# Attention in the middle of a fused macaron block: tokens normalised one batch ahead, products kept in their own batch, routing operands in PSUM, a third home for the probabilities

## The reference

```python
x = x + 0.5 * ffn(layernorm(x))
x = x + attention(layernorm(x))
x = x + 0.5 * ffn(layernorm(x))

# attention, for each batch b of 1024 tokens, width 128, causal
Q, K, V = x @ Qw, x @ Kw, x @ Vw
attn = softmax(Q @ K.T / sqrt(128) + causal_mask)
out = attn @ V

# ffn: 16 experts of 64, a router that takes 4 of 16 (from 2 of 4 groups), one shared expert of 128
scores = sigmoid(x @ Wg.T); cw = topk weights, scaled by 2.5
y = sum_e cw[:, e] * relu(x @ W1[e].T)**2 @ W2[e].T + relu(x @ Ws1.T)**2 @ Ws2.T
```

## Time and profile before

| | us |
|---|---|
| median of 3 runs (708.24 to 709.76) | 709.67 |
| the profiled execution's own time | 709.15 |
| its span, first to last instruction | 707.2 |
| PE busy in the span | 644.9 (91%) |
| DVE busy | 577.7 (82%) |
| ACT busy | 569.7 (81%) |
| POOL busy | 537.6 (76%) |

### The profile page before, as it was taken

One profiled execution on the slowest core, in us unless ns is written; L12 is line 12 of the kernel. 1 busy time (PEld: TensorE's weight loads), 2 busy tenths in 40 slices (PEclk: granted clock), 3 DMA queues, 4 the chain that ended last, 5 costly groups with the idle time before them and its releaser, 6 DMA issues.

```text
span 707.2 us, 15309 instructions
## 1 busy us (share of the span) xinstructions
PE 644.9 (91%) x3395; PEld 500.1 (71%) x3395; DVE 577.7 (82%) x2597; ACT 569.7 (81%) x1198; POOL 537.6 (76%) x427
## 2 busy tenths in 40 slices
PE   4789999999999997888888778689999999999997
PEld 4567777777777766676766666567777777777775
DVE  5998989898889895677687768988989898898863
ACT  3588889889888878888798767548898888888885
POOL 3389889989899876676556645547888998898885
PEclk9999999999999998899999999999999999999999
DMA  9857676677757712664555446953887778867783
GB/s 246 192 124 158 150 161 138 138 155 157 149 122 158 164 38 47 111 105 92 89 110 107 94 80 121 200 124 65 174 166 168 156 171 177 172 137 163 160 184 77
DMA packets 129305, 97.30 MB, mean 138 GB/s; under 512 B 80992, under 2 KB 94960, under 8 KB 129264
## 3 DMA queue, kind: packets, MB, share of 16 engines
q1 hardware_dynamic: 127056, 96.24, 66.6%
q10 hardware_dynamic: 2208, 0.59, 0.4%
HBM read 72.70 MB, written 5.24 MB: 110 GB/s over the span
## 4 chain that ended last, share of the span: by engine, by line
PE 38%; DVE 13%; ACT 5%; issue 4%; POOL 3%; DMA 1%; POOLq 0%; DVEq 0%; ACTq 0%; SPq 0%
PE psum L1319 10%; PE psum L1320 9%; PE psum L1321 9%; DVE raw_max L1190 4%; ACT zn L738 2%; PE psum L1392 2%; DVE x_sb L1223 1%; DMA wb<-scratch 1%; PE psum L1350 1%; POOL shared L518 1%; PE psum L1404 1%; PE psum L1543 1%; PE psum L1544 1%; PE psum L1545 1%; DVE s_sb L1059 1%
## 5 line engine op out<-in xcount | busy, mean ns | idle before, releaser
L430 POOL TENSOR_TENSOR shared_r<-shared,shared_r 128x512 fp32r<-128x512 f32 x256 | 326.7, 1299 | 54.2 <-ACT shared L614 51.9
L1059 DVE SCALAR_TENSOR_TENSOR s_sb<-psum,wb 128x512 f32<-128x512 f32 x256 | 175.6, 688 | 48.0 <-PE psum L1321 23.8
L614 ACT ACTIVATE shared<-s_sb 128x512 f32<-128x512 f32 x288 | 178.0, 620 | 23.1 <-DVE s_sb L1059 23.0
L613 ACT ACTIVATE shared_r<-s_sb 128x512 fp32r<-128x512 f32 x256 | 159.9, 624 | 42.0 <-DVE s_sb L1059 40.8
L518 POOL TENSOR_TENSOR shared<-s_sb,shared 128x128 f16<-128x128 f32 (+3 forms) x64 | 81.9, 1281 | 73.1 <-ACT shared L544 72.6
L1319 PE MATMUL psum<-x_hi,w_hi 128*128 128x512 f32 x288 | 127.9, 444 | 6.9 <-ACT s_sb L725 4.1
L1319 PE MATMUL psum<-shared_r,w_hi 128*128 128x512 f32 x256 | 115.1, 450 | 0.7 <-POOL shared_r L430 0.5
L1320 PE MATMUL psum<-x_lo,w_hi 128*128 128x512 f32 x288 | 115.4, 401 | 0.0
L1321 PE MATMUL psum<-x_hi,w_lo 128*128 128x512 f32 x288 | 114.3, 397 | 0.0
L1321 PE MATMUL psum<-shared_r,w_lo 128*128 128x512 f32 x256 | 101.4, 396 | 0.0
L1320 PE MATMUL psum<-shared_r,w_hi 128*128 128x512 f32 x256 | 101.1, 395 | 0.0
(11 more groups left out here) (198 smaller groups left out, 1387.7 us busy)
## 6 DMA issues: line engine op xcount, KB each, us to landing
wb<-scratch SPq DMA_DIRECT2D x128, 512.0 KB, 8.1
out<-x_sb SPq DMA_DIRECT2D x16, 256.0 KB, 9.9
x_sb<-in_L_attn_x SPq DMA_DIRECT2D x4, 256.0 KB, 6.1
scratch<-wT SPq DMA_DIRECT2D x32, 32.0 KB, 1.9
w_raw<-in_L_ffn_W ACTq DMA_DIRECT2D x1, 512.0 KB, 5.8
w_raw<-in_L_ffn_W SPq DMA_DIRECT2D x1, 512.0 KB, 6.8
w_raw<-shared SPq DMA_TRANSPOSE x32, 2.9
wb<-shared SPq DMA_TRANSPOSE x32, 3.9
```

Source lines behind the costliest of these rows:

```text
L430: nc.gpsimd.tensor_tensor(g_lo[:, j % RING, :], g_f[:, j % RING, :], g_hi[:, j % RING, :].bitcast(F32), ALU.subtract).then_inc(F.glo_done, 1)
L613: nc.scalar.activation(g_hi[:, j % RING, :], s_sb[:, j % RING, :], ACT.Square)
L614: nc.scalar.activation(g_f[:, j % RING, :], s_sb[:, j % RING, :], ACT.Square).then_inc(F.sq_done, 1)
L1059: ins = nc.vector.scalar_tensor_tensor(s_, h_, 0.0, wb[:, u, c, :], ALU.max, ALU.mult)
```

## The change

It touches attention, the groups of the second FFN that are started inside it, and where their operands lie.

- `zn` has two homes (the second in a part of `wb` that attention leaves free). ACT normalises all 8 tiles of batch b+2 at t = 0 of batch b, in one piece, for b = 1 to 5, and batches 1 and 2 inside batch 0. The statistics on DVE (t = 5 to 7) and the inverse root on POOL (t = 7) stand at the end of the batch before.
- The 16-bit high half of the tokens moves from ACT to POOL (`z16_halves`, a copy and a subtraction for each half batch), at t = 0 and 1.
- `mix(b, 0)` and `mix(b, 1)` run at t = 6 and 7 of their own batch (only batch 0's stay in batch 1). `values(b-2, 1)` moves from t = 7 to t = 0 of the next batch.
- `prob` has three homes instead of two, so `exp(m)` waits for `prob_lo(m-3)` instead of `prob_lo(m-2)`. `rsum` has three too.
- Batch b+1's q uses the same bank as its z (the spare bank 5 goes to the router), so `score(4)` waits for `q_lo_part` of half 0.
- The router's operands of groups 0 and 1 lie in PSUM bank 5, those of group 2 on in `v_ps`. The tables of k move, and groups 0 and 1 are transposed 2 and 9 tiles after they were normalised, in place of one. Their transposes and products go to `misc_ps`, and PE waits at t = 0 of batches 3 to 8 until that bank is read (`foreign`).

The diff, cut to its core:

```diff
+        prob_own = sb("prob", [P, S])
...
-        zn = sb("zn", [P, QT, D])
+        zn_own = sb("zn", [P, QT, D])
+        zn = [zn_own, wb[:, 0].rearrange("p c n -> p (c n)")[:, QT * D:2 * QT * D].rearrange("p (t d) -> p t d", t=QT)]
...
-        PF = 2
+        PF = 3
+        prob = [prob_s[:, 0:S], prob_s[:, S:2 * S], prob_own]
...
-        on_sb, on_ps = RouteTiles(rt_sb[:]), RouteTiles(v_ps)
+        on_ps, on_spare = RouteTiles(v_ps), RouteTiles(tr_ps)
...
-            z_home = psum[:, 1 + 2 * half, :]
-            return z_home, spare_ps if half == 0 and b < B - 1 else z_home
+            return psum[:, 1 + 2 * half, :]
...
+                def z16_halves(b, half):
+                    pool.wait_ge(A.zn_done, 2 * b + half + 1)
+                    wait(pool, A.mix_done, 4 * (b - 2))
+                    ts = slice(half * HQ, (half + 1) * HQ)
+                    z, z16 = zn[b % 2][:, ts, :], zn16[b % 3]
+                    nc.gpsimd.tensor_copy(z16[:, 0, ts, :], z).then_inc(A.z16hi_done, 1)
                     pool.wait_ge(A.z16hi_done, 2 * b + half + 1)
+                    nc.gpsimd.tensor_tensor(z16[:, 1, ts, :], z, z16[:, 0, ts, :], ALU.subtract).then_inc(A.z16lo_done, 1)
...
-                        if t == 5 and b + 2 < B:
-                            attention_inv(b + 2)
+                        if t == QT - 1 and b + 3 < B:
+                            attention_inv(b + 3)
                         prob_lo(b, t)
-                        if t in ((2, 3) if b > 0 else (3, 4)) and b + 1 < B:
-                            z16_lo(b + 1, t - (2 if b > 0 else 3))
+                        if b == 0 and t in (1, 2):
+                            z16_halves(0, t - 1)
+                        if b == 0 and t == 2:
+                            attention_inv(2)
+                        if b == 0 and t in (4, 5):
+                            z16_halves(1, t - 4)
+                        if 0 < b < B - 1 and t < 2:
+                            z16_halves(b + 1, t)
...
-                            if b == 0 and t < 2:
-                                normalise_tokens(1, t)
-                            if b + 1 < B and t in z16_at:
-                                z16_hi(b + 1, z16_at.index(t))
-                            if b + 2 < B and t >= 6:
-                                normalise_tokens(b + 2, t - 6)
+                                normalise_tokens(1)
+                            if t == 4 and b == 0:
+                                normalise_tokens(2)
+                            if t == 0 and 0 < b < B - 2:
+                                normalise_tokens(b + 2)
...
-                    for n, slots in ((0, {-23: (0,), -18: (1,), -17: (2,), -15: (3,), -10: (4,), -9: (5,), -7: (6,), -2: (7,), -1: (8,), 1: (9,)}),
+                    for n, slots in ((0, {-16: (0,), -14: (1,), -13: (2,), -8: (3,), -6: (4,), -5: (5,), -3: (6, 7), -2: (8,), 0: (9,)}),
...
-                                     (2, {14: (0, 1), 15: (2, 3), 16: (4, 5), 17: (6,)})) if phase == 1 else (
+                                     (2, {16: (0, 1), 17: (2, 3), 18: (4, 5), 19: (6,)})) if phase == 1 else (
...
+                            if t == 4 and 0 < b < B - 1:
+                                q_lo_part(b + 1, 1 - u, 1, prep_ps(b + 1, 1))
                             row_max(b, t, u)
...
+                            if t == 0 and 0 < b < B - 2:
+                                shift_by(b + 2)
+                            if t == 1 and b > 1:
+                                finish(b - 2, 1)
...
-                    if t == HQ + 1 and 0 < b < B - 1:
-                        pe.wait_ge(A.qlo_done, 2 * b + 4)
+                    if t in (HQ, HQ + 1) and 0 < b < B - 1:
+                        pe.wait_ge(A.qlo_done, 2 * b + t - 1)
+                    if t == HQ and b == B - 1:
+                        pe.wait_ge(N1.xf_done, 3)
...
+                            if 0 < b < B - 1 and t < 2:
+                                pe.wait_ge(A.exp_done, QT * b + t - 1)
+                                z_transpose(b + 1, 1 - u, t, prep_ps(b + 1, t))
+                            if b == 1 and t == 0:
+                                mix(0, 0)
+                                mix(0, 1)
+                            if t == 0 and b > 1:
+                                foreign(b)
+                                values(b - 2, 1)
+                            if t == 2 and b > 0:
+                                mix(b - 1, 2)
+                            if t in (2, 3) and 0 < b < B - 1:
+                                q_product(b + 1, 1 - u, t - 2, prep_ps(b + 1, t - 2))
+                            if t == 3 and b > 0:
+                                values(b - 1, 0)
+                            if t in (4, 5) and b > 0:
+                                mix(b - 1, 3, t - 4)
+                            if t in (6, 7) and b > 0:
+                                mix(b, t - 6)
```

More of the change, by code:

```diff
@@ L790, in run @@
                         sc.wait_ge(A.pT_in[r], 16 * 2 * B)
-                    for c in range(AHEAD - 1):
+                    lead_ffn(0)
+                    start_ffn(17)
+                    for c in range(1, AHEAD):
                         lead_ffn(c)
                     uT_copy(B - 1, 1)
-                    lead_ffn(AHEAD - 1)
                 return begin, run
@@ L884, in ffn, with mv_home @@
                 N_ROUTE = sum(STEPS)
-                def home(g, beyond):
-                    return on_sb if phase == 1 and isinstance(g, int) and g <= beyond else on_ps
+                def mv_home(g):
+                    return rt_mv[:] if phase == 1 and isinstance(g, int) and g <= PREP else on_ps.mv
                 def bias_copy(tiles):
@@ L921, in route @@
                     score = scores[:, u]
-                    T = home(g, PREP - 2)
-                    first_on_ps = PREP - 1 if phase == 1 else 0
+                    T = on_spare if phase == 1 and isinstance(g, int) and g < UN else on_ps
+                    first_on_ps = UN if phase == 1 else 0
                     def do(ins):
@@ L1276, in run @@
[L1276 to L1283 removed]
+                            if t in (1, 2) and b == 0:
+                                stats(2, t - 1)
@@ L1607, in run @@
                             if b > 0:
                                 start_ffn((b - (B - 2)) * QT + t)
-                    b, u = B - 1, (B - 1) % UN
-                    mix(b, 0)
-                    mix(b, 1)
+                    b = B - 1
+                    foreign(B)
+                    values(b - 1, 1)
+                    pe.wait_ge(A.exp_done, QT * B - 1)
+                    lead_ffn(0)
+                    lead_ffn(1)
+                    start_ffn(16)
                     pe.wait_ge(A.exp_done, QT * B)
-                    lead_ffn(0)
+                    lead_ffn(2)
```

247 lines of the change are left out of this document (111 added, 136 removed).

## The result

The changed kernel is slower: 724.6 us (median of 4 runs, 723.1 to 725.1) against 709.2 for the kernel before (4 runs beside them on the same chip, 708.2 to 709.8). The ratio is 1.0215, interval 1.0194 to 1.0235. The forecast was 701.7, range 690 to 710. The profiled execution took 723.09 us, its span 721.3; before it was 709.15 and 707.2.

The account below looks back on a forecast made before the run. No engine fills a batch: waits in the loop score, maximum, exponential and a slower PE clock bound it. From 709.15 us, +3.0, -2.8, -4.4, -4.6 and +1.0 make -7.8: 701.4, with 0.5 about 701.7; range 690 to 710.

Parts of the forecast that it names:

- The shift: DVE's shift ahead of ACT's normalisation: behind `prob_lo(7)` in half of the batches, 1.5 us longer each, 0.75 on average.
- The end of the root, E + 2.4: POOL's inverse root, estimated from DVE's last maximum, 0.8 us of statistics and 1.64 us for the root.
- E: The start of a middle batch's last exponential, from which the prediction laid out the batch.
- The stop at q, 2.5 us: PE, through at E + 5.2, waits for z until E + 7.7, replacing the 1.93 us stop at the transpose.
- From q to the end of the batch, 15.1: PE's remaining work from E + 7.7: batch ends at E + 21.0, 22.5 with the slow stretch, plus 0.3 router work.
- Batches 2 to 5, 94.2 us: Four middle batches of attention, 97.0 us before, at 22.5 + 0.75 + 0.3 each: -2.8 us, bounds -12 to +2.
- The slow rival: Normalising eight tiles behind the late shift stops PE 4 us each batch; batches 2 to 5 at 24.6, about 716; chance 0.12.
- The router's groups: In batches starting a router group, PE's 2.26 us stop for tokens goes; 0.3 us of ACT's normalisation counted.
- Batches 0 and 1, +3: POOL's 16-bit halves, copies taken at 1.0 us, delay the roots in batch 0: +3 us, bounds 0 to +6.
- Batch 6, -4.4: No normalisation piece, so no stop at q: 21.5 us for 25.9, bounds -6 to -1.
- Batch 7, -4.6: Window loses about 4 us of DVE work, so PE bounds it: 20.0 us for 24.6, bounds -6 to -1.
- The tail, +1.0: After the last exponential, router group 2's parts stand before the second and third gate: +1.0 us, bounds 0 to +3.

Follow-up runs that it names:

- the moments in PSUM: The changed kernel with the means and variances of batches 2 to 7 in PSUM and no instruction moved: 714.4 us, ratio 1.0067.
- late pairs: The changed kernel with batches 1 to 5's shift at t = 2 and normalisation two tiles each at t = 3 to 6: 707.5 us, ratio 0.9976.
- the best version: Changed kernel with moments in PSUM, late pairs, router shifts two tiles later, mix pairs 0 and 1 back, router group 0's last part later: 694.4 us, ratio 0.9789.
- a version without the stops: Changed kernel with moments in PSUM, late pairs and router shifts two tiles later (698.4 us); two homes for the probabilities instead of three gave 700.6 us.

## Why the prediction was wrong, step by step

The step that failed is "The shift", and through it the layout of a middle batch. The wait for the shift was to be 1.5 us in half of the batches, 0.75 on average. It was 2.3 to 2.65 in every one.

- **The end of the root, E + 2.4.** It was E + 3.8 (E = 372.37). I timed the root by its input on DVE and left out what stands ahead of it in POOL's own queue: `prob_lo(6)`, 1.90 us, which can start only when ACT's copy of tile 6 is done, 0.1 us behind E. 0.1 + 1.9 + 1.64 was to be had before the run, from the order of the queues and the durations of the profile.
- **The shift late in half of the batches, 1.5 each.** With the root at E + 3.8 it was behind `prob_lo(7)` in every batch that has a root: ACT waited 2.65, 2.27, 2.65 and 2.50 us for it in batches 2 to 5. `prob_lo(7)` is ready at E + 2.3, as forecast, so the order of the two was no matter of chance. I had made it an even one.
- **The stop at q, 2.5 us.** It was 5.2, 3.4, 5.2 and 5.0 in batches 2 to 5. ACT's piece began at E + 5.97 for the E + 2.9 of the forecast. PE was through at E + 5.7 (forecast 5.2). Less ACT's wait for the shift, the stop is 2.5 in batches 2, 4 and 5. So up to the product q everything but the shift was right within 0.5.
- **From q to the end of the batch, 15.1 (13.3 at full clock, 1.5 for the slow stretch, 0.3 for the router's work).** It took 15.7 and 16.3 us in batches 4 and 5, and 16.6 and 17.3 in 2 and 3. Of the 14.5 us by which the four batches went over 94.2, some 9 lie ahead of q and some 5.5 behind it. The stops of the router's shifts are in the latter for batches 2 and 3; for 4 and 5 the excess is 0.6 and 1.2 and stays open.
- **Batches 2 to 5, 94.2 us.** They took 108.7, outside my bounds of -12 to +2. The slow rival had the right mechanism and the right sign of its threshold (stops of 4 us), and was also too short: 24.6 a batch against 27.2. It lacked the stops of the router's shifts, of which moving that shift alone takes 4.3 us off batch 3 and nothing off batch 2. Batches 4 and 5, which have none, took 26.6 and 26.7.
- **The router's groups.** I gave their batches 0.3 us of ACT's work and took the stop of 2.26 in the earlier trace rows as gone. It went, and DVE's wait for the root took its place: 2.34 us in batches 2 and 3 of the changed kernel, 3.27 in batch 7. I had counted what POOL does, and not what DVE queues behind a wait for POOL. PE's wait of 2.31 in batch 3 for the shared bank was not counted either.
- **Batches 0 and 1, +3.** They took +4.9, inside the bounds. The copy on POOL takes 0.61 us, not 1.0 (row below), so that reason is too dear. What the runs show is: the shift blocked in batch 0 is worth 1.0 (22.4 to 21.4 with the moments in PSUM), the halves ahead of the root 0.9 more (20.5 with the root earlier), and late pairs take 3.5 off batch 1 (25.0 to 21.4). Batch 0 was 19.2 before the change, and the last 1.3 stay open.
- **Batch 6, -4.4.** It came to -2.8, with the wait of 5.08 for the second root in it. I had written that it has no stop at q; it had one of 2.86. Moved away, in the best version, that wait leaves a batch of 19.4.
- **Batch 7, -4.6.** It came to -0.6, with the group 2 shift in it (5.35 us of DVE). With that shift moved, on the changed kernel, the batch takes 20.6 (forecast 20.0). So this term was right about the work and wrong about the wait.
- **The tail, +1.0.** It was -0.3 from the last exponential to the end.
- **"Nothing" for the third home.** Likely 2.5 us in a version without the stops; in the changed kernel it was not tried. The trace before shows no such wait, but POOL had no 16-bit copies then.
- **The last line.** 701.4 and 0.5 are 701.9, not 701.7; nothing hangs on it.

The copy, in the rows of the changed kernel (count, busy, mean ns):

```profile
L518 POOL CAST zn<-wb 128x512 f16<-128x512 f32 x6 | 3.7, 613 | 0.0
```

Half of the price of the subtraction in the earlier trace rows. The Trainium skill (GPSIMD Engine Reference, section "Engine selection") puts one-input work of GpSimd at roughly line rate and two-input work at about twice VectorE's time. The 0.6 us that the prediction took from it and did not use was a better guide than the nearest row of the same engine.

What stays open: why batches 2 and 3 still take 23.6 and 23.7 in the best version, where the others from batch 5 on take 19.4 to 20.8. In batch 2 the stop of 3.63 us at the router's transposes is a part of it. ACT is busy 19 to 20 us in both. An attempt to clear this was not made. Nor was batch-ahead normalisation undone by itself, so its own worth is not measured; the experiments only show what its place cost.

## What to carry to other kernels

When a small operation of GpSimd is moved, time it by what stands ahead of it in GpSimd's queue as well as by its input, and look what GpSimd starts next: here a small VectorE operation on SBUF that began 0.07 us behind it took as long as that (2.08 us for 2.12), and 0.17 with an operand in PSUM. Put the consumer of a GpSimd result behind the place where it could first run (two tiles were enough here), since everything that the engine has queued behind it waits too. Then check the next consumer in line: the same move left the router's tokens too late for their transpose. When two estimated times are 0.1 us apart and their order decides, the forecast is not done: work both out from the queues, or price the bad order in full.

## What the runs showed of the hardware

- A VectorE scaling with one input, 128x8 floats from SBUF to SBUF, took 1.69 us beside a GpSimd instruction that had begun 0.24 us before it, 0.17 with no GpSimd instruction running, and 0.17 beside one with its input in PSUM. On 128x64 another such operation took 1.16, 0.19 and 0.22.
- GpSimd's power of 128x8 floats takes 1.64 us and of 128x4 1.01, more than its copy of 128x512 to 16 bits at 0.61. A root counts as a large instruction in GpSimd's queue.
- In the changed kernel the stops of PE of 4.94, 5.19, 5.20 and 5.04 us ahead of the product q were followed by a granted clock of 0.50 to 0.52 in the next three us, the one of 3.40 by 0.73, and the one of 2.31 at the start of batch 3 by 1.00. In the best version, with one stop of over 3 us left, five of six windows from batch 2 on have 0.98 to 1.00.
